# Three parts instead of two in the last plan of a routed layer, and bank sums opened by a transposition

## What is computed

```python
x = x + attention(layernorm(x))      # 16 heads, 4 key groups, head width 16, causal, RMS norm, rotation
x = x + ffn(layernorm(x))            # 8 experts of width 176, the best 2 of each token
x = x + memory(layernorm(x))         # 4 banks of linear memories, weighted by a softmax, then Wo
x = x + ffn(layernorm(x))            # the same experts again

# ffn
probs = softmax(x @ Wr); topk_w, topk_idx = top_k(probs, 2); topk_w /= topk_w.sum()
y = sum over the two experts e of a token:  w_e * ((silu(x @ Wg[e]) * (x @ Wu[e])) @ Wd[e])

# memory, per bank n and head h
sigma = elu(x @ Wq.T) + 1
out = sum_n softmax(bank_weights)[h, n] * (sigma @ M[n, h]) / (sigma @ norm[n, h])
```

## Time and profile before

| | us |
|---|---|
| median of 3 runs | 531.05 |
| the runs | 529.84, 531.05, 535.29 |
| the profiled execution, its own time | 530.55 |
| its span, first to last instruction | 528.8 |

### The profile page before, as it was taken

The page is one execution under the profiler, slowest core; times in us unless marked ns, Lnnn a source line. Parts: engine busy times, 40 slices in busy tenths (PEclk is TensorE's granted clock), DMA queues, the critical chain, the costliest instruction groups (busy, mean ns, idle before and its releaser), DMA issues.

```text
span 528.8 us, 10970 instructions
## 1 busy us (share of the span) xinstructions
PE 481.9 (91%) x3380; PEld 327.6 (62%) x3380; DVE 373.1 (71%) x1098; ACT 269.1 (51%) x642; POOL 248.8 (47%) x308
## 2 busy tenths in 40 slices
PE   7998999999999999899999979999979998899960
PEld 3545665765765676666777636675747775677740
DVE  5999989889999866754345657868867675344473
ACT  4577898887887874333333415524223532334320
POOL 5519339238750062473423655446473756343330
PEclk9999999999999999999999999999989999999995
DMA  6572800111130432374335492012132357433585
GB/s 198 212 281 120 176 21 10 54 58 47 61 99 4 117 115 72 116 196 131 102 110 160 78 190 42 34 38 72 49 106 86 130 162 194 120 98 113 161 296 168
DMA packets 43736, 60.77 MB, mean 115 GB/s; under 512 B 5856, under 2 KB 38240, under 8 KB 43040
## 3 DMA queue, kind: packets, MB, share of 16 engines
q1 hardware_dynamic: 33696, 38.24, 24.4%
q0 software_dynamic: 9984, 21.83, 13.9%
HBM read 28.89 MB, written 25.00 MB: 102 GB/s over the span
## 4 chain that ended last, share of the span: by engine, by line
PE 58%; DVE 10%; DMA 5%; issue 4%; ACT 3%; POOL 2%; SPq 1%; POOLq 0%; DVEq 0%; ACTq 0%
PE PS L1140 14%; PE PS L1157 9%; PE PS L1186 4%; PE PS L1027 4%; PE PS L1004 3%; PE PS L1149 3%; PE PS L1195 3%; PE PS L1121 3%; PE PS L1089 2%; DMA ys<-yo,xin 2%; PE PS L1203 2%; PE PS L1167 2%; DVE smax L1479 2%; DMA kbd<-ys 2%; PE PS L1078 2%
## 5 line engine op out<-in xcount | busy, mean ns | idle before, releaser
L1878 POOL DMA_INDIRECT ys<-yo,xin x78 | 75.2, 964 | 104.7 <-DVE yo L1700 95.4
L1140 PE MATMUL PS<-wexp,xTt 128*128 x312 | 105.2, 464 | 2.7 <-issue 1.5
L1479 DVE TENSOR_REDUCE smax<-PS 128x1 f32<-128x512 f32 (+3 forms) x176 | 102.2, 632 | 6.3 <-PE PS L1006 5.8
L1305 ACT ACTIVATE prob<-PS 128x512 f16<-128x512 f32 (+1 forms) x176 | 92.7, 562 | 20.3 <-PE PS L1029 19.0
L1863 POOL DMA_INDIRECT xs<-xn,pos x64 | 62.5, 977 | 57.9 <-DVE pos L1574 40.8
L1157 PE MATMUL PS<-wexp,hT 88*128 x312 | 80.4, 384 | 2.3 <-ACT hT L1355 2.1
L1140 PEld LDWEIGHTS PS<-wexp,xTt 128*128 128x128 f32 x312 | 54.7, 190 | 24.9 <-issue 5.2
L1687 DVE SCALAR_TENSOR_TENSOR sg<-th,PS 128x176 f32<-128x176 f32 x78 | 26.2, 336 | 58.1 <-ACT th L1349 57.9
L1349 ACT ACTIVATE th<-PS 128x176 f32<-128x176 f32 x78 | 24.7, 317 | 82.5 <-PE PS L1140 82.5
L1157 PEld LDWEIGHTS PS<-wexp,hT 88*128 88x128 f32 x312 | 55.4, 189 | 15.2 <-issue 4.4
L1027 PE MATMUL PS<-qT,kbd 128*128 128x512 f16 (+3 forms) x256 | 60.8, 299 | 2.2 <-ACT qT L1297 1.0
(11 more groups left out here) (210 smaller groups left out, 845.2 us busy)
## 6 DMA issues: line engine op xcount, KB each, us to landing
xin<-xs SPq DMA_DIRECT2D x78, 129.0 KB, 2.1
kbd<-ys SPq DMA_DIRECT2D x20, 256.0 KB, 4.4
wexp<-in_experts SPq DMA_DIRECT2D x4, 1216.0 KB, 9.3
xs<-zeros SPq DMA_DIRECT2D x32, 129.0 KB, 4.1
xn<-xn SPq DMA_DIRECT2D x8, 512.0 KB, 3.3
xall<-ys POOLq DMA_DIRECT2D x6, 512.0 KB, 6.9
out<-xall SPq DMA_DIRECT2D x8, 256.0 KB, 2.7
kbd<-kT SPq DMA_DIRECT2D x60, 32.0 KB, 1.9
```

The costliest lines, as they stand in the source:

```text
L1140: mm = pe.matmul(PS[:, bank, 0:2 * FI], xTt[:, j % NXT, kc * P:(kc + 1) * P], wexp[:, bass.ds(expert[f, j], 1), kc * 2 * FI:(kc + 1) * 2 * FI]
L1305: act.activation(prob[:, u % NPR, 0:nr * w], PS[:, bank, 0:nr * w], ACT.Exp, scale=ATT_SCALE)\
L1479: dve.tensor_reduce(smax[:, i, REP * g + r0:REP * g + r0 + nr], PS[:, bank, 0:nr * w].rearrange("p (r w) -> p r w", r=nr), AX.X, ALU.max). ...
L1878: pool.indirect_dma_start(ys[f], bass.IndirectOffsetOnAxis(xin[:, j % NXIN, D + 1:D + 2].bitcast(I32), axis=0), yo[:, j % NYO], None).then ...
```

## The change

1. `tiles_with` takes the half: of batch 3, half 0 now needs only tile 34 (`MIXED_HALF` is 35), half 1 still tile 38. For this the last plan has 24 segments instead of 16: the rows of batches 0 to 2, those of the first half of batch 3, those of the second half.
2. `count` for the last plan adds five small matmuls (the counts up to the middle of batch 3).
3. The plan's comparisons, products and sums grow with the segments. The constant `upto` (16x16 values per partition) is no longer loaded, but built by two DVE instructions of 24x24 in piece 0 of the first plan. `pl_mask` and `upto` are in bf16.
4. In the planner's description, and so in the orders, the second half of a fetch is only `behind` the first half; before, it was `after` it, and the planner counted the first one's 3.3 us of landing. This holds for all five joined batches. Costs, ranks and `NUDGE` stay as they are.
5. In `combT` the first of the two products is a PE transposition (`pe.transpose`), the second adds to it.

```diff
+MIXED_HALF = (2 * (B - 1) * S + S) // P + NE - 1
+SEGS = 3 * NE
...
+def tiles_with(b, h=1):
+
+    return MIXED if b < B - 1 else TILES if h else MIXED_HALF
...
-            w.add(SP, rank + 0.1 * k, 0.75, "fetch", f, b, k, after=rows + ([(DVE, "join", *JOINED[n - 2], 1)] if n >= 2 else [])
-                  + [(SP, "fetch", f, b, 0)] * k, lands=3.3)
+            w.add(SP, rank + 0.1 * k, 0.75, "fetch", f, b, k, after=rows[k] + ([(DVE, "join", *JOINED[n - 2], 1)] if n >= 2 else []),
+                  behind=[(SP, "fetch", f, b, 0)] * k, lands=3.3)
...
+                        if batches == B:
+
+                            for c in range(B - 1):
+                                pe.matmul(PS[:, bank, NE:2 * NE], ones_b[:], part[:, c], start=(c == 0), stop=False)
+                            for i in range(NT // 2):
+                                mm = pe.matmul(PS[:, bank, NE:2 * NE], ones_b[:], chosen[:, B - 1, i], start=False,
+                                               stop=(i == NT // 2 - 1))
...
-                            for n in range(2):
-                                mm = pe.matmul(PS[:, bank, kc * P:(kc + 1) * P], scl[:, u % 4, n], ident_f,
-                                               start=(n == 0), stop=(n == 1))
+                            o = PS[:, bank, kc * P:(kc + 1) * P]
+                            pe.transpose(o, scl[:, u % 4, 0], ident_f)
+                            mm = pe.matmul(o, scl[:, u % 4, 1], ident_f, start=False, stop=True, skip_group_check=True)
...
+                        if piece == 0 and n == 0 and f == 0:
+
+                            row, column = late["tiles"][:, 0:SEGS].unsqueeze(2), late["tiles"][:, 0:SEGS].unsqueeze(1)
+                            link(dve.tensor_tensor(upto[:], column.to_broadcast([P, SEGS, SEGS]),
+                                                   row.to_broadcast([P, SEGS, SEGS]), ALU.is_le))
+                            link(dve.tensor_scalar(upto[:], upto[:], float(P), None, ALU.mult))
...
-                            link(dve.tensor_tensor(pl_cmp[:], count.unsqueeze(2).to_broadcast([P, NE, 16]), steps,
+                            link(dve.tensor_tensor(more, counts.unsqueeze(3).to_broadcast([P, 2, NE, 16]),
+                                                   late["steps"].unsqueeze(1).unsqueeze(1).to_broadcast([P, 2, NE, 16]),
                                                    ALU.is_gt))
-                            dve.tensor_reduce(pl_tmp[:], pl_cmp[:], AX.X, ALU.add).then_inc(taken[bank], 1)
+                            dve.tensor_reduce(pl_need[:], more, AX.X, ALU.add).then_inc(taken[bank], 1)
...
+                            dve.tensor_tensor(pl_tiles[:, 2 * NE:], pl_need[:, 0], pl_need[:, 1], ALU.subtract)
+                            dve.scalar_tensor_tensor(pl_hi[:, 2 * NE:], pl_need[:, 0], float(P), late["base"],
+                                                     ALU.mult, ALU.add)
```

More of the change, by code:

```diff
@@ L455, in combine @@
 def combine(w, f, b, rank):
-    done = tiles_with(b)
-    rows = [(POOL, "down", f, j) for j in range(done - NYO, done)]
+    rows = [[(POOL, "down", f, j) for j in range(tiles_with(b, h) - NYO, tiles_with(b, h))] for h in range(2)]
     n = JOINED.index((f, b)) if (f, b) in JOINED else None
@@ L907, in _ @@
                         f, b, h = a
-                        for j in range(tiles_with(b) - NYO, tiles_with(b)):
+                        for j in range(tiles_with(b, h) - NYO, tiles_with(b, h)):
                             wait_for_row(sp, f, j)
@@ L1609, in _ @@
                         if piece == 0:
-                            link(dve.tensor_tensor(pl_sum[:, 0:segs, 0:segs], own.unsqueeze(1)
-                                                   .to_broadcast([P, segs, segs]), late["upto"][:, 0:segs, 0:segs],
+                            link(dve.tensor_tensor(sums, own.unsqueeze(1)
+                                                   .to_broadcast([P, segs, segs]), upto[:, 0:segs, 0:segs],
                                                    ALU.mult))
-                            link(dve.tensor_reduce(pl_upto[:, 0:segs], pl_sum[:, 0:segs, 0:segs], AX.X, ALU.add))
+                            link(dve.tensor_reduce(pl_upto[:, 0:segs], sums, AX.X, ALU.add))
                         elif piece == 1:
@@ L1942 @@
         "before": f(p[:, None] < p[None, :]), "steps": rows(P * np.arange(16), 16),
-        "upto": rows(P * (seg[None, :] <= seg[:, None]), SEGS, SEGS), "tiles": rows(P * np.arange(JL), JL),
+        "tiles": rows(P * np.arange(JL), JL),
         "next_expert": rows(np.append(np.diff(seg % NE), 0), SEGS),
```

24 lines of the change are left out of this document (14 added, 10 removed).

## The result

Changed kernel: 535.69 us, median of 20 runs (531.37 to 538.92). Kernel before, beside it: 532.3 us, median of 20 runs (528.99 to 535.29). The ratio, which is not simply the quotient of the medians (that is 1.0064, or 3.4 us), is 1.0049, 95% interval 1.0027 to 1.0071: about 2.6 us slower, within 1%. The forecast was 529.4 with a range up to 535.0. It had the direction wrong and the time outside the range, by 0.7 us; the kernel before itself is 1.25 us higher here than in the three runs that the forecast started from. Ratios leave out the few executions in a slower state of the chip; medians count them.

The account below looks back on a forecast made before the run. PE was taken to bind in the memory stage, PE and DVE together in attention, transfer order at the end. Terms -3.0 +1.8 +0.7 +0.7 -1.5 -0.3 = -1.6 from 530.55 gave 528.95, 529.4 on the median's footing; range 523.5 to 535.

Parts of the forecast that it names:

- The larger plan: Last plan of each layer: 2.2 us more DVE work; first layer +1.8 us, second layer +0.7, building upto +0.7.
- the second layer: Second layer's last plan: delay mostly taken back by PE's later idle time, no load late; +0.7 us, bounds 0 and 2.2.
- the build of `upto`: Attention: two added DVE instructions, at most 1.5 us, half hidden by slack; +0.7 us, bounds 0 and 1.5.
- The transposition: Bank sums in the memory stage: half the products become transpositions, saving PE time; -3.0 us, bounds -3.5 and 0.
- The prediction's own sign of being wrong: Memory stage: PE's idle time away from 4 us by more than 3 would show the forecast wrong.
- The orders, first layer: Transition into the memory stage: earlier second joins let its latency chain start sooner; -1.5 us, with reshuffle -4 to +3.
- Rival (a): Memory stage: the new order leaves PE waiting for DVE and POOL; +8 us, 537.4; chance 0.13.
- (c): Whole kernel: all gains come and DVE's growth is hidden; -9.0 us, 522; chance 0.14.
- The end: Tail: one fetch fewer after the last scatter saves 2.7, joins delay that scatter 2.6; net -0.3, bounds -2.8 and +3.0.
- rival (b): Tail: joins with late data stall the last tiles; +3.0 us at the end instead of -0.3, 532.7; chance 0.17.
- Rival (e): Tail: SP's in-order list makes fetch (3, 0) no earlier; end gives nothing or +2.6, 529.7 to 532.3; chance 0.10.
- Rival (d): Memory stage: transpositions bring half-clock dips, one more for each batch; +5.6 us, 535; chance 0.05.

Follow-up runs that it names:

- before_order: Kernel before with only the planner's rule for the second half of a fetch changed (behind instead of after); 533.06 us, ratio 1.0004.
- before_turn: Kernel before with only the first product of each combT made a PE transposition; 531.87 us, ratio 1.0000.
- plan_only_third: Kernel before with only the larger plan, old products, fetch rule and order of work, on the first kind of chip; 536.92 us beside 534.79, ratio 1.0035.

## Why the prediction was wrong, step by step

**The larger plan: right in its cost, too low in the second layer.** 0.75 us for 576 values was worked out, 0.75 measured. PE's wait was to grow to 3.8 us and grew to 3.62. Attention lost 0.5 us to the build of `upto` (0.7 predicted). All plans together: +3.2 predicted, +2.1 (1.1 to 3.1) measured over both kinds, +1.9 (0.2 to 3.6) on the first. In the second layer no load was late, as said, but the delay of PE in front of the pads was not taken back by its idle time further on: the ledger has +2.0 instead of +0.7, near the upper bound of 2.2, with the clock at 0.90 in 447 to 456. Over that stretch the five profiled kernels of the first kind with the larger plan lose 2.0 to 3.8 us against before, the two with the old plan (before_order, before_turn) 0.4 and 0.6.

**The transposition: the step that failed.** The term was -3.0, bounds -3.5 and 0; measured 0.0, plus or minus 1.7, on the first kind. The cost of the instructions was right to the hundredth. Wrong was the step from "PE binds" in the memory stage (PE busy 83.77 of 88 us) to a saving of which only 0.5 us is lost in waits. DVE is busy 66 us there, and with a little less PE work the chain that ended last went through DVE for about 26 us instead of 13, and PE waited longer. That is how the chains look; no run with a faster DVE stage tests it. The bound at 0 was there; the value taken stood at the wrong end of it. The prediction's own sign of being wrong, PE's idle time away from 4 us by more than 3, came true with 7.4, though part of it is there without the transposition.

**The orders, first layer: half right.** PE's busy time between 300 and 316 rose from 12.34 to 15.65 in the changed kernel, as said. By the ledger of before_order 1.6 us came out at the end of the memory stage; the term was -1.5. Rival (a), +8 from the reshuffle, did not come, nor did (c), in which every gain comes. On the whole kernel the new rule gave 0.2 us plus or minus 1.8, since the same rule costs about 2 us at the end.

**The end: one piece too small.** The order of the joins came exactly as worked out, and gate_up 36 and 38 slipped. The last scatter was to slip by 2.6 us; behind the second plan it slipped by 5.3 (+3.4 to +8.8). What was taken at nothing is the wait for the joins' data. DVE waited 1.21 and 0.53 us for it ahead of gate_up 36 and 0.53 ahead of gate_up 38, together 2.27 of the 2.7 us that the forecast lacks, and the fetches with 5.35 and 5.03 us are the largest pieces of the chain that ended last. This is the mechanism of rival (b). What stands behind the last scatter shrank by 4.5 (10.8 us instead of 15.3), more than the 2.7 predicted, and so the net is +0.9 instead of -0.3, and (b)'s +3.0 did not come. Two misses of the forecast partly cancel here; that is luck. Rival (e) did not come: the fetch of (3, 0) was issued at 518.56, ahead of the last scatter. The prediction also wrote down that the load of tile 38 goes behind all four fetches, and gave it no term. The load is not on the chain of the changed kernel, but it comes next: with the joins ranked late, it is the largest piece there (5.90 us), PE stands 2.58 us for it, and the end is no sooner by the ledger (+0.9 again).

**The sum.** By the ratios, first kind: plans +2.1, transposition 0.0, rule 0.2; together +2.3, and the changed kernel has +2.6. The forecast had +3.2 for the plans and -4.8 for all the rest. Of the 4.2 us between -1.6 and +2.6, 3.0 are the transposition's term; the plans came 1.1 cheaper, and the orders and the end together 2.3 dearer. No gain of the early half can be read from the rest, 0.3 us with an uncertainty near 3. On the second kind, on one chip, the plans cost 2.9 (1.0050) and all the rest gives 3.7 back, which leaves the -0.8 measured. Why the same 3.5 us of PE work pay there and not on the first kind is open; the stops described below make PE later against DVE and POOL, which would leave more of the memory stage to PE, but this is a guess, and no run isolates it.

**The clock.** Not settled in full. Rival (d) had dips in the memory stage; there the clock stayed 0.98. The slow L1186 at 387.17 that it took as its example stands behind a wait of 3.02 us for DVE's `qa`, not behind transpositions. A dip to 0.77 behind the first plan was seen, its cost by the ledger of one execution 3 us, and it was my main theory after the result. Four runs speak against it as a cost of the change: before_order has a dip at the same place with the old plan, taking the dip away by filler gave no net gain, lengthening the stop cost no more than the work although the clock fell to 0.76 behind it, and plan_only_third, with the longer stop, has a mean clock of 0.977 over 12 runs beside 0.975 for before. On the other side, the 20 runs of the changed kernel have a mean of 0.973, 0.004 below the 33 of before; by 3.7 us for 0.01 that would be 1.4 of its 2.6 us, and no run tells what lowered it; the clocks of the 20 runs of before beside it are not on record, and on another chip of the same kind before has 0.975 itself. Dips come with the old plan and with the larger one, in varying places; what a profile of one execution shows of them belongs to that execution.

## What to carry to other kernels

A saving on an engine that is busy 95% of a stage is worth what the next engine's slack allows, so look up how much of the stage's chain belongs to that engine and what stands right behind it before you credit the saving. When an edit moves transfers in a queue that is worked off in order, price when the data of each one lands, both for the instructions that wait for the moved ones and for the loads that end up behind them. Once the first wait is removed, the next one bounds the time. Measure a few us against medians: two profiled executions of one kernel can differ by more than the change.

## What the chips showed that I had not expected

**Two kinds of chip.** The same kernel before takes 532 to 535 us on two chips and 577 to 581 on two others. DVE's busy time is equal (373.1 and 372.2 us); PE's is not, and it stands still where the profile names no releaser. PE in order of time on the second kind, at 208 us; in before on the first kind no single wait of PE for "issue" is longer than 0.6 us:

```profile
208.13 0.61 PE L1027 MATMUL PS<-qT,kbd 128*128 128x512 f16 x1 [4.63 <-issue]
```

PE's waits for "issue" on the second kind, by line (total us, times, longest), first two:

```profile
PE PS L1157 <- issue: 10.6, 7, 3.4
PE PS L1027 <- issue: 9.1, 6, 4.6
```

The clock is at half behind such a stop (0.61 us for a product of 512 columns that takes 0.38 otherwise), and its mean is 0.943 instead of 0.977. What the stops are isn't shown.

**Executions and clock.** On one chip, 33 executions of the kernel before went with their mean granted clock: about 3.7 us less for each 0.01 more. That the two go together does not say which causes the other, and filler that raised the clock at one place did not lower the time.
